# A two-layer graph network on one core: row turns in pairs, each engine's body reordered to match, first loads on one queue, two result stores later

## The reference

```python
h = jnp.maximum(_layernorm(x), 0.0)
A = relu((adj + adj.T) * 0.5)                      # layer 0
d = where(A.sum(1) > 0, A.sum(1) ** -0.5, 0)
x = x + relu((eye - d[:, None] * A * d[None, :]) @ (h @ W0))
h = jnp.maximum(_layernorm(x), 0.0)                # layer 1, three weights
x = x + diag(adj) @ (h @ W1[0]) + triu(adj, 1) @ (h @ W1[1]) + tril(adj, -1) @ (h @ W1[2]) + bias
```

## Time and profile before

| | |
|---|---|
| time, median of 3 runs | 951.08 us (949.88 to 952.29) |
| profiled execution: time, span | 951.66 us, 949.9 us |
| TensorE busy | 911.5 us, 96% of the span |
| VectorE, ScalarE, GpSimd busy | 59%, 51%, 31% |
| mean granted TensorE clock | 0.987 |
| a steady step of layer 0, first half and second half | 16.7 us, 13.6 us |
| VectorE busy from 58 to 90 us, in the start | 30.4 of 32 us |
| chain that ended last | TensorE 89%, VectorE 4%, DMA 3%, ScalarE 2% |

### The profile page before, as it was taken

The page is one execution under the profiler, slowest core; times in us unless marked ns, Lnnn a source line. Parts: engine busy times, 40 slices in busy tenths (PEclk is TensorE's granted clock), DMA queues, the critical chain, the costliest instruction groups (busy, mean ns, idle before and its releaser), DMA issues.

```text
span 949.9 us, 17218 instructions
## 1 busy us (share of the span) xinstructions
PE 911.5 (96%) x4471; PEld 769.6 (81%) x4471; DVE 564.7 (59%) x1475; ACT 488.3 (51%) x1026; POOL 289.9 (31%) x300
## 2 busy tenths in 40 slices
PE   3688999999999999999999999899999999999998
PEld 2568878888888888888888888688888888888886
DVE  4999777878787776565656565344444333344332
ACT  3887567676666765545554554243343333333331
POOL 4894444434434443443444332011111100000000
PEclk9789999999999999999999999999999999999999
DMA  9995999999999986556555653766565655555552
GB/s 284 325 289 149 302 320 334 337 334 339 330 341 327 325 312 181 158 178 198 162 159 177 199 186 120 229 192 186 189 193 183 204 165 165 166 160 160 165 169 67
DMA packets 179578, 212.69 MB, mean 224 GB/s; under 512 B 13648, under 2 KB 114000, under 8 KB 177488
## 3 DMA queue, kind: packets, MB, share of 16 engines
q1 hardware_dynamic: 134160, 156.87, 54.3%
q10 hardware_dynamic: 45376, 55.32, 16.7%
HBM read 143.99 MB, written 68.16 MB: 223 GB/s over the span
## 4 chain that ended last, share of the span: by engine, by line
PE 89%; DVE 4%; DMA 3%; ACT 2%; issue 1%; ACTq 0%; DVEq 0%; SPq 0%
PE psAcc L578 24%; PE psAcc L576 24%; PE psAcc L577 24%; PE psA L452 3%; PE psG L547 2%; PE psG L549 2%; PE psG L548 2%; PE psZ L487 2%; PE psW L422 1%; DVE sring L919 1%; DMA colb<-in_adj 1%; DMA xp<-in_x 1%; DMA x<-in_L_gnn_W 1%; PE psAcc L590 1%; PE psAcc L589 1%
## 5 line engine op out<-in xcount | busy, mean ns | idle before, releaser
L650 ACT ACTIVATE Lh<-C 128x512 fp32r<-128x512 f32 x256 | 161.1, 630 | 267.8 <-PE psAcc L578 201.4
L576 PE MATMUL psAcc<-Xh,Lh 128*128 128x512 f32 x496 | 199.8, 403 | 2.7 <-DVE Xl L1063 2.6
L576 PE MATMUL psAcc<-Yh,Lh 128*128 128x512 f32 x512 | 200.9, 392 | 0.0
L578 PE MATMUL psAcc<-Yh,Ll 128*128 128x512 f32 x512 | 200.1, 391 | 0.0
L577 PE MATMUL psAcc<-Yl,Lh 128*128 128x512 f32 x512 | 199.9, 390 | 0.0
L578 PE MATMUL psAcc<-Xh,Ll 128*128 128x512 f32 x496 | 194.7, 393 | 0.0
L577 PE MATMUL psAcc<-Xl,Lh 128*128 128x512 f32 x496 | 194.0, 391 | 0.0
L850 DVE TENSOR_TENSOR Ll<-C,Lh 128x512 fp32r<-128x512 f32 x128 | 95.7, 748 | 129.7 <-ACT Lh L650 129.5
L578 PEld LDWEIGHTS psAcc<-Yh,Ll 128*128 128x128 f32 x512 | 96.1, 188 | 20.3
L577 PEld LDWEIGHTS psAcc<-Yl,Lh 128*128 128x128 f32 x512 | 96.2, 188 | 18.9
L576 PEld LDWEIGHTS psAcc<-Yh,Lh 128*128 128x128 f32 x512 | 96.2, 188 | 18.6
(11 more groups left out here) (140 smaller groups left out, 1356.0 us busy)
## 6 DMA issues: line engine op xcount, KB each, us to landing
C<-at_dram SPq DMA_DIRECT2D x128, 256.0 KB, 2.8
at_dram<-AT SPq DMA_DIRECT2D x16, 1088.0 KB, 5.6
s_dram<-C ACTq DMA_DIRECT2D x64, 256.0 KB, 5.1
R<-in_adj SPq DMA_DIRECT2D x64, 256.0 KB, 5.7
g_dram<-g ACTq DMA_DIRECT2D x32, 512.0 KB, 3.6
C<-s_dram SPq DMA_DIRECT2D x64, 256.0 KB, 3.9
C<-in_adj SPq DMA_DIRECT2D x60, 256.0 KB, 5.2
t_dram<-x ACTq DMA_DIRECT2D x32, 256.0 KB, 2.3
```

The source lines that it names most:

```text
L576: mm(acc, lh, rh[:, k, :], start=k == 0, stop=False)
L578: mm(acc, ll, rh[:, k, :], start=False, stop=c < L1 and k == NB - 1).then_inc(used, 1)
L650: A(Lh[:, q, :], C[:, q, :], ACT.Relu if s.c < L1 else ACT.Copy).then_inc(lhi, 1)
```

## The change

- **First loads.** The four first blocks of x, W0 and layer 1's weights were issued by ScalarE, beside SyncE's loads; now SyncE issues them all, each block of x behind a chunk of the matrix. The rounding of the weights (Wh on ScalarE, Wl on VectorE), which stood first on both engines, moves to slots 5 and 7 of the start.
- **Row turns.** For steps 1 to 15 TensorE turned one strip after each strip it multiplied; now two after strip 1 and two after strip 3.
- **Bodies.** ScalarE and VectorE no longer copy, sum and split strip by strip between other work, but strips 0 and 1 of the next step together late in a step, and strips 2 and 3 early in the step that needs them. The turn of xp moves behind G0 and G1.
- **Stores.** In steps 33 and 34 SyncE's `store_out` moves from the start of the body to its end.

```diff
@@ sync
                                  cols_v[k, :, 4 * g:4 * g + w, :]).then_inc(ld_first[g], 16)
+                    if g < TILES_WITH[0]:
+                        load_tiles([g])
...
             load_first()
+            sp.dma_start(W0[:, :], w_l0).then_inc(ld_w, 16)
+            sp.dma_start(x1[:, 0, 0:3 * F].rearrange("p (k o) -> p k o", k=3),
+                         w_l1.rearrange("k f o -> f k o")).then_inc(ld_w, 16)
...
-                if c > L1:
+                if c > L1 + 2:
                     store_out(t)
...
                 if L1 <= c < L1 + 2:
                     load_t(t)
+                if L1 + 1 <= c <= L1 + 2:
+                    store_out(t)
@@ tensor
-                if k == 11 and c < NB:
-                    wait(pe, p_h, t.of(1, 1))
...
-                    turn(xp, yT)
                 if k in (11, 14) and 2 <= c < L1 + 2:
...
+                if k == 11 and c < NB:
+                    wait(pe, p_h, t.of(1, 1))
...
+                    turn(xp, yT)
...
                         finish(t, k)
-                    if c < NB:
+                    if c < NB and q % 2:
+                        rows_T(Step(t.i, c + 1), q - 1)
                         rows_T(Step(t.i, c + 1), q)
@@ scalar
+                if 2 <= c <= NB:
+                    copy_T(t, 2)
+                    copy_T(t, 3)
+                    rectified_sum(t)
+                    split_hi(t, 2)
                 split_hi(t, NQ - 1)
...
-                if c < NB:
-                    copy_T(nxt, 0)
-                if c == 1:
+                if 1 <= c <= 2:
                     normal_xp(t)
-                if c < LAST - 1:
+                if NB <= c < LAST - 1:
                     split_hi(nxt, 0)
...
-                if 2 <= c < NB:
+                if 3 <= c < NB:
                     normal_xp(t)
...
                 if c < NB:
+                    copy_T(nxt, 0)
                     copy_T(nxt, 1)
+                    split_hi(nxt, 0)
                 if c < LAST - 1:
                     split_hi(nxt, 1)
-                if c < NB:
-                    copy_T(nxt, 2)
...
-                if c < LAST - 1:
+                if NB <= c < LAST - 1:
                     split_hi(nxt, 2)
...
-                if c < NB:
-                    copy_T(nxt, 3)
@@ vector
+                if 2 <= c < NB:
+                    sum_T(t, 2)
                 if 1 <= c < NB:
                     sum_T(t, NQ - 1)
...
+                if 2 <= c <= NB:
+                    split_lo(t, 2)
                 split_lo(t, NQ - 1)
...
-                if c < NB - 1:
-                    sum_T(nxt, 0)
...
                 if c < NB - 1:
+                    sum_T(nxt, 0)
                     sum_T(nxt, 1)
                 if 1 <= c <= L1:
                     wait(dve, x1_ok, t.of(1, 0))
                     stats(ne, x1[:, pe_, :], e_st, e_mv, e_ve, t.of(1, 0))
-                if c < LAST - 1:
+                if c < NB:
+                    split_lo(nxt, 0)
+                elif c < LAST - 1:
                     split_lo(nxt, 1)
...
-                if c < NB - 1:
-                    sum_T(nxt, 2)
...
-                if c < LAST - 1:
+                if c < NB:
+                    split_lo(nxt, 1)
+                elif c < LAST - 1:
                     split_lo(nxt, 2)
```

More of the change, by code:

```diff
@@ L206, in build @@
         SLOTS = range(-1, 56)
+        WEIGHTS_AT = 5
         BY_DVE = 4
@@ L531, in finish @@
                     turn(h2, hT)
-                if k == 11 and c < NB:
-                    wait(pe, p_h, t.of(1, 1))
-                    if c >= 2:
-                        wait(pe, hThi, t.of(1, -1))
-                        wait(pe, hTlo, t.of(1, -1))
-                    else:
-                        wait(pe, yT_ok, t.of(1, 0))
-                    turn(xp, yT)
                 if k in (11, 14) and 2 <= c < L1 + 2:
@@ L549, in finish @@
                         mm(psG[:, b % 2, 0:3 * F], hTl[:, f], Wh[:, :], start=False, stop=True).then_inc(g_ok, 1)
+                if k == 11 and c < NB:
+                    wait(pe, p_h, t.of(1, 1))
+                    if c >= 2:
+                        wait(pe, hThi, t.of(1, -1))
+                        wait(pe, hTlo, t.of(1, -1))
+                    else:
+                        wait(pe, yT_ok, t.of(1, 0))
+                    turn(xp, yT)
             def body(t):
@@ L597, in _ @@
             A = nc.scalar.activation
-            for j in range(TILES_WITH[0]):
-                act.dma_start(blocks(hst[:, node(j), :]), xv[0, node(j)]).then_inc(ld_x0[j], 16)
-                if j == 0:
-                    act.dma_start(W0[:, :], w_l0).then_inc(ld_w, 16)
-                    act.dma_start(x1[:, 0, 0:3 * F].rearrange("p (k o) -> p k o", k=3),
-                                  w_l1.rearrange("k f o -> f k o")).then_inc(ld_w, 16)
-            act.wait_ge(ld_w, 32)
-            A(Wh[:, :], x1[:, 0, 0:3 * F], ACT.Copy).then_inc(whi_ok, 1)
             act.wait_ge(const0, 2)
@@ L685, in _ @@
                     rectify(n)
+                if n == WEIGHTS_AT:
+                    act.wait_ge(ld_w, 32)
+                    A(Wh[:, :], x1[:, 0, 0:3 * F], ACT.Copy).then_inc(whi_ok, 1)
                 for j in range(NB):
@@ L728, in body @@
                     A(g2h[:, :], g2[:, :], ACT.Copy).then_inc(g2h_ok, 1)
-                if c < NB:
-                    copy_T(nxt, 0)
-                if c == 1:
+                if 1 <= c <= 2:
                     normal_xp(t)
-                if c < LAST - 1:
+                if NB <= c < LAST - 1:
                     split_hi(nxt, 0)
-                if 1 <= c <= L1:
-                    wait(act, z_ok, t.of(1, 0))
-                    if c >= 3:
-                        wait(act, st_t[pe_], t.pair(-1, 16))
-                    elif c == 1:
-                        act.wait_ge(wlo_ok, 1)
-                    A(x1[:, pe_, :], z[:, :], ACT.Relu, scale=cur_e[:, 2:3]).then_inc(r1_ok, 1)
+                if c == 1 or NB < c <= L1:
+                    rectified_sum(t)
                 if 1 <= c <= NB:
@@ L793, in body, with rectified_sum @@
                     act.dma_start(strip(g_dram, t, 2), g12[:, :, :].rearrange("p k w -> p (k w)")).then_inc(st_g, 16)
+            def rectified_sum(t):
+                c, pe_ = t.c, (t.c - 1) % 2
+                wait(act, z_ok, t.of(1, 0))
+                if c >= 3:
+                    wait(act, st_t[pe_], t.pair(-1, 16))
+                elif c == 1:
+                    act.wait_ge(wlo_ok, 1)
+                A(x1[:, pe_, :], z[:, :], ACT.Relu, scale=cur_e[:, 2:3]).then_inc(r1_ok, 1)
             def prep(t):
@@ L852, in _ @@
             V.memset(drow[:, :, :], 0.0).then_inc(d_zero, 1)
-            dve.wait_ge(whi_ok, 1)
-            V.tensor_tensor(Wl[:, :], x1[:, 0, 0:3 * F], Wh[:, :].bitcast(F32), ALU.subtract).then_inc(wlo_ok, 1)
             dve.wait_ge(d_zero, 1)
@@ L924, in _ @@
                     chunk_sum(n)
+                if n == WEIGHTS_AT + 2:
+                    dve.wait_ge(whi_ok, 1)
+                    V.tensor_tensor(Wl[:, :], x1[:, 0, 0:3 * F], Wh[:, :].bitcast(F32), ALU.subtract).then_inc(wlo_ok, 1)
                 for e in range(len(GROUPS)):
```

## The result

The changed kernel takes 976.77 us (median of 6 runs, 972.55 to 981.98) against 950.31 for the kernel before beside it: ratio 1.0284, 95% interval 1.0263 to 1.0304. The forecast was 947.1. The profiled execution took 972.55 us, with a span of 970.8 against 949.9: +20.9. It was the shortest of the six, so the traces show 21 of the 26 us.

A forecast was written before the change was run, and what follows sets the result against it. TensorE's instruction stream was taken as the bound in layer 0's first half, with DMA a close second limit. Terms -4.6 - 0.4 + 1.1, the rest 0, summed to -3.9 us; forecast 947.1 us, range 943.5 to 951.5.

The forecast's parts named there:

- The bodies in a steady step: First-half steady steps: G2 finds its buffer free with 0.2 us to spare; 0, at worst 4 us lost in all.
- Stores: Steps 33 and 34: later store_out frees the loads, removing step 35's wait and slow clock; -4.6 us, bounds -2.6 to -4.9.
- Pairs: Row turns two at a time: -0.03 us for each of 13 steps, -0.4 us, bounds 0 and -1.
- Step 1 to 2: Start of step 2: strip 0's Ll comes late for TensorE; +1.1 us, bounds 0.6 and 1.5.
- Step 2: In step 2, G0 waits for hTh in place of the turn of xp; 0, bounds -1.7 and +0.6.
- First loads: Start: VectorE's earlier start is used up by TensorE's fifth chunk awaiting the same bytes; 0, bounds -1.5 and +1.
- Rival A: Every first-half step loses 0.15 to 0.5 us as G2 awaits gev_out or G0 awaits hTl; 949 to 953 us; chance 0.22.
- Rival B: First-half steps: strip 1's row load R comes late, 0.6 to 1 us a step; 955 to 960 us; chance 0.08.
- Rival C: New gaps before and in step 2 slow TensorE's clock, +1.9 to +3.7 us; 949 to 951 us; chance 0.06.
- E: Steps 33 and 34: moved stores bring nothing since load_t blocks SyncE at the same place; 951 to 952 us; chance 0.04.
- D: Start or step 2 gains too, -1.5 from load order or -1.7 from its wait; 943.5 to 945.8 us; chance 0.12.

The follow-up runs named there:

- e_bodies: Changed kernel with its first loads and two stores put back as before, leaving paired row turns and new bodies: 980.62 us, ratio 1.0327.
- e_stores: Kernel before with only store_out of steps 33 and 34 moved behind the other loads: 946.86 us, ratio 0.9964.
- e_unpair: Changed kernel with row turns back to one strip at a time, bodies as changed: 977.27 us.
- e_loads: Kernel before with only the first loads and the weights' loads and splits moved: 949.72 us, ratio 0.9992.
- e_issue_xr: Changed kernel with rectified sum put back but in its own tile, strip 1's R early, ScalarE's strip 1 store and xp load behind gev 1: 965.70 us.
- e_xr: Changed kernel with the rectified sum at its new early place but written to a tile of its own: 970.79 us.
- e_r1late: Changed kernel with the rectified sum of steps 2 to 16 put back to just ahead of Yh: 970.10 us.
- e_xpturn: Changed kernel with rectified sum put back, strip 1's R early and the turn of xp back ahead of G0 and G1: 966.19 us.
- e_at4: Changed kernel with rectified sum put back, strip 1's R early and AT's 1088 KB store as four transfers together at its place: 957.66 us.

## Why the prediction was wrong

**The failed step is "The bodies in a steady step", taken as 0.** It costs 30 us (e_bodies): a steady step takes 18.49 us and not 16.7. I added up the chain from the turn of h2 to G2 and looked at nothing ahead of it: "Early in a step all is well: strips 2 and 3 are split by about 6 us". That sentence left out the wait inside `rectified_sum`. In step 9 of the changed kernel, which starts at 240.61, ScalarE has split them 8.3 and 8.8 us in, and VectorE's second Ll ends 10.6 us in. The diff moves the call to the head of the body; the kernel has `wait(act, st_t[pe_], ...)` in that function and issues this store in the last lines of the body before; the earlier trace rows gave 5.1 us for a store of this size. Put into the sum, it would have read: issue at the end of a body, 5 us to landing, x wanted some 2 us on (read from the changed kernel's step 9), so about 3 us of waiting in ScalarE in each of 13 steps, 40 us on an engine that idled 62 of 190 us. It measured 46.2 us in 13 steps. This wait is the part of the failed step that the runs show best, 6 to 6.7 us given back without it and 17.6 lost by it alone in the old bodies; the rest of the 30 us lies in other delays of the same order of work, below. I had asked of each added instruction what it waits for, but not of this moved one.

- Stores, -4.6: the mechanism and the place are right, to the earlier trace rows are gone. Sized by the trace -4.4, by e_stores -3.4 (the interval is 2.1 to 4.7 us).
- Pairs, -0.4: nothing to be seen (e_unpair); too small to be told.
- Step 1 to 2, +1.1: right, and nearer (0.02 us) than its bounds of 0.6 and 1.5 could promise, which is luck. TensorE waits 1.12 us for Ll at the head of step 2:

```profile
111.99 0.47 PE L584 MATMUL psAcc<-Xh,Lh 128*128 128x512 f32 x1 [1.12 <-DVE Ll L857]
```

- Step 2, 0: nearly right. A wait of 1.9 us for hTl ahead of G0 replaces that of the earlier trace rows; a wait of 0.4 us for R comes on top.
- First loads, 0: right. The wait of the earlier trace rows is gone and the first chunk starts at 5.77 us, but the fifth starts only at 20.26, after a wait, against 21.40, and e_loads measured -0.5 us, inside its interval of -1.6 to +0.1. That agrees with the rule of the Trainium skill (DMA: Bandwidth & Descriptors, "Issuing engines are not separate DMA queues") that the same 16 DMA engines carry the transfers of either engine.
- Rival A: its mechanism is there and its price was right for each step (some 0.5 us of G2's wait in e_issue_xr, where ScalarE waits for no store; 5.8 us given back by VectorE's order). It was the smaller part of the 30 us.
- Rival B: its mechanism is there (nine waits for R), its price alone is nothing and 3.5 us with the sum repaired, which is not clear of the scatter. I put the issue 7.6 us ahead of the turn; it was 5.9, since the chain of ScalarE ahead of it was late.
- Rival C: not seen in the changed kernel. Its waits of up to 1.9 us were followed by no slow matmuls, clock 1.00 from 98 to 390 us, as the wait of the earlier trace rows had been. In six of the experiments it did fall between 125 and 400 us, in e_xr three times. The Trainium skill (TensorE: Matmul & The Clock Gate, "Part 1: The HAM clock gate") ties the clock to recent activity; the traces agree in that the falls of e_xr, e_r1late and e_xpturn come with a wait of TensorE of 1.79 to 3.21 us.
- E is out; of D, the wait in step 2 did not go. Its lower end should have read 943.9 (947.1 - 1.7 - 1.5), not 943.5.

The account of the 30 us: with the sum put back 6.7 come back, with R early 3.5 (not clear of the scatter), with AT's store in four 8.9, and VectorE's order gave 5.8 in another version, which it only brought back to the time of e_at4. From 957.66 us (e_at4) to 946.23 it is 11.4 us, and their cause stays open. VectorE's order may be a piece of them, but e_at4 with that edit alone was not run. Open too are why moving the issues or giving the sum its tile helps in one version and hurts in the next, and what in e_at4 beside the shorter issues gives the rest of its 8.9; VectorE's wait for xp is a candidate for both, untested.

## What to carry to other kernels

For every instruction that a change moves forward, list its waits, find where each awaited thing is issued, and put issue + landing + the new distance into the sum; a store that is issued last in a loop body speaks against an early place for its buffer's next writer. Where TensorE is busy all of a steady step and three other engines serve it in order, a wait of 3 to 5 us at the head of an in-order body reaches everything behind it, and repairing one such wait shows the next: judge a reordering by the whole, and size its parts by adding them one at a time to the good version, not only by taking them from the bad one. And when a change bundles a local fix with a reordering, time the fix alone first.

## What the runs showed of the hardware

- The time that ScalarE needs to issue a 256 KB transfer depends on what has just been issued: 0.34 to 0.42 us as a rule, 0.8 to 1.66 us for xp's, the second or third of ScalarE's in the 1 to 4 us behind SyncE's store of 1088 KB, and 1.20 to 1.54 for the one before it in half of the steps. ScalarE's work stands still meanwhile (24 us before yTs in 14 steps). Cutting the store into four at the same place brings the mean of the xp load from 1.12 to 0.94 us, spreading it out to 0.42 (in a version whose steps are also longer).
- From issue to landing, the AT store went from 5.5 to 7.5 us (median, 125 to 375 us) and the xp load from 5.9 to 8.4, while the DMA engines moved less (302 against 319 GB/s in that stretch): fewer bytes in the same time, and each transfer longer under way. Why, no run here shows.
- TensorE's granted clock does not follow from the length of the last wait alone. It stayed at 1.00 behind waits of up to 1.93 us in the changed kernel, 2.55 in e_bodies and 2.42 in e_r1late (at 322.53), and fell behind waits of 2.57 before, of 2.42 (at 358.88) in e_r1late and of only 1.79 in e_xpturn (275 to 278 us, first row below). In e_xr, 210 to 230 us hold a wait of 3.06 us for R, and the clock is 0.91 on average there (second row):

```profile
275.00:278.00 3.00, 3.00 (x13) 2.60 (x12) 2.48 (x6) 1.64 (x6) 1.28 (x1) 0.50 1.01 302
```
```profile
210.00:230.00 20.00, 17.21 (x84) 14.88 (x85) 14.36 (x39) 10.91 (x23) 7.14 (x10) 0.91 0.98 299
```
